# Recommendation tower: gram products in two bursts a tile, a GpSimd wait three chunks ahead, eleven look-ups in every unit, last unit tile by tile

## The reference, cut to what matters

```python
# ids [2048, 27]; 27 tables of 128 columns (1000 to 125000 rows)
e = stack([tbl_f[ids[:, f]] for f in range(27)], axis=1)      # [2048, 27, 128]
z = einsum('bnd,bmd->bnm', e, e)[:, c, r]                     # 351 pairs below the diagonal
h = concatenate([z, dense_ctx], axis=1)                       # [2048, 367]
h = maximum(h @ W_top1 + b_top1, 0)                           # 512 columns
h = maximum(h @ W_top2 + b_top2, 0)                           # 256 columns
y = h @ W_top3                                                # [2048, 1]
```

## Time and profile before

| | |
|---|---|
| time, median of 3 runs | 360.29 us (360.21 to 361.26) |
| profiled execution, first to last instruction | 358.7 us |
| TensorE matmuls busy | 333.7 us, 93% |
| VectorE busy | 246.3 us, 69% |
| GpSimd busy | 250.4 us, 70% |
| ScalarE busy | 144.4 us, 40% |
| mean granted TensorE clock | 0.986 of full speed |

### The profile page before, as it was taken

How to read it: one execution, slowest core, us unless ns; L and a number is a source line. 1 busy time by engine, 2 the same in 40 slices (tenths; PEclk the granted TensorE clock), 3 DMA queues, 4 the chain that set the end, 5 groups by cost and what they waited for, 6 DMA issues and landing times.

```text
span 358.7 us, 13616 instructions
## 1 busy us (share of the span) xinstructions
PE 333.7 (93%) x6094; PEld 303.4 (85%) x6094; DVE 246.3 (69%) x329; ACT 144.4 (40%) x265; POOL 250.4 (70%) x271
## 2 busy tenths in 40 slices
PE   1879699989999989999999999999999999999896
PEld 0779499978999979898889989999899989997775
DVE  3959979975488935878197965968387955961142
ACT  2536524444433433335343453435343353435320
POOL 5777777777777777777777777777777777777200
PEclk9969989999999999999999999999999999999999
DMA  6997744534333353443333452434533443322100
GB/s 184 306 318 196 205 136 107 102 93 91 83 93 82 90 99 75 96 96 80 93 88 82 115 85 77 105 84 81 102 89 83 99 98 74 84 55 55 27 3 1
DMA packets 26155, 36.86 MB, mean 103 GB/s; under 512 B 8451, under 2 KB 20099, under 8 KB 26098
## 3 DMA queue, kind: packets, MB, share of 16 engines
q0 software_dynamic: 8448, 17.32, 20.5%
q1 hardware_dynamic: 17506, 18.16, 20.1%
q10 hardware_dynamic: 144, 0.52, 0.4%
HBM read 35.97 MB, written 0.01 MB: 100 GB/s over the span
## 4 chain that ended last, share of the span: by engine, by line
PE 57%; POOL 26%; issue 10%; DVE 3%; DMA 3%; ACT 1%; DVEq 0%; ACTq 0%
POOL rows L450 26%; PE e_banks L482 25%; PE w_banks L543 9%; PE g_banks L513 8%; PE w_banks L554 7%; PE e_banks L494 6%; DMA rows<-in_tbl,idx 2%; DVE one_hot L672 2%; PE w_banks L532 1%; DVE zt L686 1%; DMA idx<-in_idx 1%; ACT et L340 0%; ACT h L333 0%; ACT et L350 0%; DVE a L720 0%
## 5 line engine op out<-in xcount | busy, mean ns | idle before, releaser
L450 POOL DMA_INDIRECT rows<-in_tbl,idx x264 | 249.6, 945 | 82.9 <-issue 78.0
L672 DVE TENSOR_TENSOR one_hot<-ids_wide,row_no 128x1024 fp32r<-128x1024 int32 x160 | 186.3, 1215 | 76.5 <-PE e_banks L482 72.5
L482 PE MATMUL e_banks<-one_hot,table_hi 128*128 128x256 f32 x672 | 172.2, 294 | 3.4 <-issue 3.4
L482 PE MATMUL e_banks<-one_hot,table_lo 128*128 128x256 f32 x672 | 167.0, 287 | 0.0
L482 PEld LDWEIGHTS e_banks<-one_hot,table_hi 128*128 128x128 f32 x672 | 131.4, 196 | 4.4 <-issue 4.2
L482 PEld LDWEIGHTS e_banks<-one_hot,table_lo 128*128 128x128 f32 x672 | 131.6, 196 | 0.2
L350 ACT ACTIVATE et<-e_banks 128x256 f32<-128x256 f32 x84 | 57.9, 689 | 89.3 <-PE e_banks L482 89.3
L340 ACT ACTIVATE et<-e_banks 128x512 f32<-128x512 f32 (+1 forms) x68 | 45.0, 664 | 52.3 <-PE e_banks L494 51.5
L513 PEld LDWEIGHTS g_banks<-et 128*26 128x26 f32 x4096 | 41.7, 103 | 17.7 <-issue 13.3
L513 PE MATMUL g_banks<-et 128*26 128x26 f32 x4096 | 50.0, 191 | 1.8 <-DVE zt L686 1.3
L494 PE MATMUL e_banks<-ident,rows 128*128 128x128 f32 x264 | 43.0, 285 | 5.5 <-DMA rows<-in_tbl,idx 5.5
(11 more groups left out here) (25 smaller groups left out, 67.7 us busy)
## 6 DMA issues: line engine op xcount, KB each, us to landing
ids_wide<-in_ids SPq DMA_DIRECT2D x80, 128.0 KB
et<-in_kept_tables SPq DMA_DIRECT2D x10, 512.0 KB, 10.1
rows<-in_tbl,idx POOLq DMA_INDIRECT x264
et<-in_kept_tables ACTq DMA_DIRECT2D x1, 512.0 KB, 3.9
a1T<-in_ids SPq DMA_DIRECT2D x4, 128.0 KB, 10.8
w<-in_w SPq DMA_DIRECT2D x2, 256.0 KB
w<-in_W_top SPq DMA_DIRECT2D x1, 512.0 KB
w<-in_w SPq DMA_DIRECT2D x1, 222.0 KB
```

The costliest lines, as they stand in the source:

```text
L450: pool.indirect_dma_start(rows[:, k % RING, a, :], None, tables[f], bass.IndirectOffsetOnAxis(ap=idx[:, t, f:f + 1], axis=0)).then_inc(row ...
L482: last = nc.tensor.matmul(e_bank[n % E_BANKS][:, 0:UNIT], part[:, q, c, :], one_hot[:, hot_slot(o, piece), c % PIECE, :], start=(c == 0 an ...
L672: nc.vector.tensor_tensor(one_hot[:, hot_slot(o, piece), :, :], ids_place(o).unsqueeze(1).broadcast_to([P, PIECE, UNIT]), row_no[:, piece ...
```

## The change

Tile t's eight gram pieces are issued as two bursts of four, at the end of the first and the third tick of tile t+1 (for tile 14 the first and the second), instead of a pair in every tick. Each burst raises `g_filled` once, and the turn waits for both. `H` steps are interleaved with look-ups and layer steps now.

GpSimd, before it gathers chunk k, waits until the transposes of chunk k-4 and all bursts that lie in ticks up to k-4 are done. The ring keeps its seven places.

`GATHERED_IN` is empty: 256 gathers, 64 chunks of four, 88 look-ups. The costs and the first tick of each unit's look-ups change, so look-ups move between ticks.

The last unit's layers are done tile by tile. Layer 1 of unit 6 is one tick, its layer 2 the next; tile 14's turning and layer 1 (`H1`, `M1`, 128 columns each) lie in the last tick. `END` holds tile 15's grams with tile 14's layer 2 between the bursts, and then tile 15's own turning, layer 1 and layer 2. For tile 15, ScalarE and VectorE take the drains in turn.

```diff
-GATHERED_IN = {0: 3, 4: 1}
+GATHERED_IN = {}
+AHEAD_BY = 3
@@ the order
-        at = 1 + (n - AHEAD) * 7 // 10
-        step = [("OH", 0, q)] + [("HI", n + AHEAD)]
+        at = 1 + (n - AHEAD) * 6 // 10
+        step = [("OH", 0, q)] + [("HI", m) for m in range(n + AHEAD, min(n + AHEAD + 1, NOH))]
...
+    HALF = G_PIECES // 2
+    BURST_AT = []
     for t in range(LAST_TILE):
         at = TILE_AT[t + 1] + (t == 0)
-        for p in range(G_PIECES):
-            step = [("G", t, p)] + ([("turn", t), ("pack", t)] if p == G_PIECES - 1 else [])
-            grams[at + p * 4 // G_PIECES].append(step)
-    for u in range(LAST):
-        at, then = TILE_AT[PAIR * (u + 1) + 1], TILE_AT[min(PAIR * (u + 2), LAST_TILE)]
+        for half, tick in enumerate((at, at + (1 if t == LAST_TILE - 1 else 2))):
+            grams[tick] += [("G", t, p) for p in range(half * HALF, (half + 1) * HALF)]
+            BURST_AT.append(tick)
+        grams[tick] += [("turn", t), ("pack", t)]
+    for u in range(LAST - 1):
+        at, then = TILE_AT[PAIR * (u + 1) + 1], TILE_AT[PAIR * (u + 2)]
         turns[at] += [[("H", u, c)] for c in range(KC)]
         layers[at + 1] += [[("L1", u, 0)], [("L1", u, 1)]]
         layers[at + 2] += [[("L1", u, 2)], [("L1", u, 3)]]
-        if u < LAST - 1:
-            layers[then].append([("L2", u, 0)])
-            layers[then + 1].append([("L2", u, 1)])
-
-    COLUMNS = {"T": 1024, "OH": 4096, "G": 1024, "H": 1024, "L1": 3072, "L2": 4096}
-    LOOK_UPS_FROM = [0, TILE_AT[1] + 1] + [TILE_AT[PAIR * (u - 1)] + 4 for u in range(2, UNITS + 1)]
+        layers[then + 1].append([("L2", u, 0)])
+        layers[then + 2].append([("L2", u, 1)])
+
+    at, tile = TILE_AT[LAST_TILE], LAST_TILE - 1
+    turns[at] += [[("H", LAST - 1, c)] for c in range(KC)]
+    layers[at + 1] += [[("L1", LAST - 1, m)] for m in range(M1)]
+    layers[at + 2] += [[("L2", LAST - 1, j)] for j in range(PAIR)]
+    layers[at + 3] += [[("H1", tile, c)] for c in range(KC)] + [[("M1", tile, m)] for m in range(M1)]
+
+    COLUMNS = {"T": 1024, "OH": 4608, "G": 768, "H": 768, "L1": 3072, "L2": 4096, "H1": 320, "M1": 1536}
+    LOOK_UPS_FROM = [0, TILE_AT[1] + 2] + [TILE_AT[PAIR * (u - 1)] + 3 for u in range(2, UNITS)] + [TILE_AT[LAST_TILE]]
...
-    END = pieces[:G_PIECES // 2] + [("L2", LAST - 1, 0)] + pieces[G_PIECES // 2:] \
-        + [("turn", LAST_TILE), ("pack", LAST_TILE), ("L2", LAST - 1, 1)] \
-        + [("H", LAST, c) for c in range(KC)] + [("L1", LAST, m) for m in range(M1)] \
-        + [("L2", LAST, j) for j in range(PAIR)]
+    END = pieces[:HALF] + [("L2", LAST, 0)] + pieces[HALF:] + [("turn", LAST_TILE), ("pack", LAST_TILE)] \
+        + [("H1", LAST_TILE, c) for c in range(KC)] + [("M1", LAST_TILE, m) for m in range(M1)] \
+        + [("L2", LAST, PAIR - 1)]
...
-        for step in look_ups[k] + layers[k]:
-            STEPS += step
-        for turn, piece in itertools.zip_longest(turns[k], grams[k], fillvalue=[]):
-            STEPS += turn + piece
+        for turn, step in itertools.zip_longest(turns[k], look_ups[k] + layers[k], fillvalue=[]):
+            STEPS += turn + step
+        STEPS += grams[k]
@@ GpSimd
-                if k >= RING:
-                    pool.wait_ge(t_filled, k - RING + 1)
+                if k > AHEAD_BY:
+                    pool.wait_ge(t_filled, k - AHEAD_BY)
+                bursts = sum(tick <= k - AHEAD_BY - 1 for tick in BURST_AT)
+                if bursts:
+                    pool.wait_ge(g_filled, bursts)
@@ TensorE
-                if p == G_PIECES - 1:
+                if p % HALF == HALF - 1:
                     last.then_inc(g_filled, 1)
...
+            def turn_tile_pairs(s):
+                _, t, c = s
+                n = W_AT[s]
+                free_w_bank(n)
+                wait_packed(t, c)
+                nc.tensor.transpose(w_bank[n % WB][0:KROWS[c], 0:P], h[:, t % PAIR, c * P:c * P + KROWS[c]], ident[:]
+                                    ).then_inc(w_filled, 1)
+
+            def layer1_tile(s):
+                _, t, m = s
+                n = W_AT[s]
+                free_w_bank(n)
+                for c in range(KC):
+                    if m == 0:
+                        w_emptied(W_AT["H1", t, c])
+                    last = nc.tensor.matmul(w_bank[n % WB][:, 0:P], w1[0:KROWS[c], c, m * P:(m + 1) * P],
+                                            hT[0:KROWS[c], c, t % PAIR, :],
+                                            start=(c == 0), stop=(c == KC - 1))
+                last.then_inc(w_filled, 1)
@@ VectorE
-                dve.wait_ge(g_filled, t + 1)
+                dve.wait_ge(g_filled, 2 * (t + 1))
```

More of the change, by code:

```diff
@@ L150, in dlrm_tower @@
         layers[at + 2] += [[("L1", u, 2)], [("L1", u, 3)]]
-        if u < LAST - 1:
-            layers[then].append([("L2", u, 0)])
-            layers[then + 1].append([("L2", u, 1)])
-    COLUMNS = {"T": 1024, "OH": 4096, "G": 1024, "H": 1024, "L1": 3072, "L2": 4096}
-    LOOK_UPS_FROM = [0, TILE_AT[1] + 1] + [TILE_AT[PAIR * (u - 1)] + 4 for u in range(2, UNITS + 1)]
-    load = [sum(COLUMNS[step[0][0]] for step in turns[k] + layers[k] + grams[k]) for k in range(TICKS)]
+        layers[then + 1].append([("L2", u, 0)])
[7 more added lines that the diff above has]
+    LOOK_UPS_FROM = [0, TILE_AT[1] + 2] + [TILE_AT[PAIR * (u - 1)] + 3 for u in range(2, UNITS)] + [TILE_AT[LAST_TILE]]
+    load = [COLUMNS["T"] + sum(COLUMNS[step[0]] for part in turns[k] + layers[k] + [grams[k][:HALF]] for step in part)
+            for k in range(TICKS)]
     for u in range(1, UNITS):
@@ L328, in w_engine, with turned_cols, layer1_cols @@
                 return "dve"
-            return "dve" if s[1] == LAST and s[2] % 2 == 1 else "act"
+            return "dve" if s[1] == LAST_TILE and s[0] in ("H1", "M1") and s[2] % 2 == 1 else "act"
+        def turned_cols(s):
+            if s[0] == "H":
+                return w_bank[W_AT[s] % WB][:, 0:UNIT].rearrange("p (j b) -> p j b", b=P), slice(0, PAIR)
+            j = s[1] % PAIR
+            return w_bank[W_AT[s] % WB][:, 0:P].unsqueeze(1), slice(j, j + 1)
+        def layer1_cols(s):
+            if s[0] == "L1":
+                return w_bank[W_AT[s] % WB][:, 0:UNIT].rearrange("p (j b) -> p j b", b=P), slice(0, PAIR)
+            j = s[1] % PAIR
+            return w_bank[W_AT[s] % WB][:, 0:P].unsqueeze(1), slice(j, j + 1)
         def copy(eng, out, src):
@@ L612, in drain_turned @@
                 act.wait_ge(w_filled, n + 1)
-                cols = w_bank[n % WB][:, 0:UNIT].rearrange("p (j b) -> p j b", b=P)
-                copy("act", hT[0:KROWS[c], c, :, :], cols[0:KROWS[c]]).then_inc(w_drained[n % WB], 1)
+                cols, tiles = turned_cols(s)
+                copy("act", hT[0:KROWS[c], c, tiles, :], cols[0:KROWS[c]]).then_inc(w_drained[n % WB], 1)
             def drain_layer1(s):
@@ L645, in _ @@
                     pack_first(s[1])
-                elif s[0] == "H" and w_engine(s) == "act":
+                elif s[0] in ("H", "H1") and w_engine(s) == "act":
                     drain_turned(s)
-                elif s[0] == "L1" and w_engine(s) == "act":
+                elif s[0] in ("L1", "M1") and w_engine(s) == "act":
                     drain_layer1(s)
@@ L749, in _ @@
                     pack_rest(s[1])
-                elif s[0] == "H" and w_engine(s) == "dve":
+                elif s[0] in ("H", "H1") and w_engine(s) == "dve":
                     drain_turned(s)
-                elif s[0] == "L1" and w_engine(s) == "dve":
+                elif s[0] in ("L1", "M1") and w_engine(s) == "dve":
                     drain_layer1(s)
```

22 lines of the change are left out of this document (14 added, 8 removed).

## The result

The changed kernel takes 368.13 us (median of 5 runs, 364.90 to 369.96) against 360.29 (5 runs, 360.20 to 361.26): ratio 1.0207, 95% interval 1.0176 to 1.0237. It is slower, as the whole interval lies above 1; whether by more than 2% stays open. The forecast was 357 us and faster, and the time lies outside the range of 352.5 to 363.

What follows compares the result with a forecast made beforehand. TensorE, busy 93%, and GpSimd, gathering without a stop, were taken as all but balanced, TensorE a little behind. 358.7 + 0.3 + 0.7 - 4.1 = 355.6 us span; median 1.6 above, 357.2; range 352.5 to 363.

Steps and rivals of the forecast that it cites:

- gaps: I take the middle, 5.0: Tile 2 to last chunk: gaps inside 28 bursts total 5.0 us against 3 before, +2.0; bounds 0 and 14.3.
- Rival 1: Bursts run dry: each long burst has 0.51 us of gaps, 14.3 instead of 5.0; time 366.5 us, slower; chance 0.14.
- Joining saves 0.23 a burst: Gram pieces: one burst of four costs 1.29 us where two pairs cost 1.52.
- To tile 2, 65.2: Start to tile 2's transposes: 64.9 us before, changes sum to +0.3, so tile 2 at 65.2.
- Waits for rows and around `H`, -3.9: Tile 2 to last chunk: row waits of 2.6 us and about 1.3 around H steps end, -3.9.
- The new wait, hidden: GpSimd loses about 5.9 us at chunks 9, 11 and 12, hidden by TensorE being later; then gathers without a stop.
- The end, 18.5: Last chunk's transposes to kernel end: 18.5 us against 22.6 before, -4.1, with last-unit records at 0.113 us.
- The end's sign: Last unit by tile: end gains 4.1 us, while unit 6's layer 2 moved into the middle costs 3.5.
- Look-ups, +5.8 here and one more ahead: Tile 2 to last chunk: 72 look-ups instead of 69, 1.92 us each, +5.8; before tile 2, one fewer, -1.92.
- Rival 3: A burst saves nothing, since each matmul has a fixed price; time 361.6 us; chance 0.08.
- Rival 4: Last unit by tile gives nothing, M1 being as dear as L1; time 361.5 us, no difference; chance 0.08.
- Rival 2: Gathers bound the kernel: gaps are small and the rows' landing sets the end; time 353 to 356 us; chance 0.20.

Runs made afterwards that it cites:

- e6: Not the kernel's computation: TensorE alternates 24 matmuls with bursts of 256 gram records on constant data, GpSimd idle, gathering or doing something else; span 167.0 us.
- e7: Gram records alone on constant data: bursts of 64, 96 and 128 with GpSimd idle, then 128 beside gathers, plain DMAs or memsets; span 236.6 us.
- e3: Changed kernel without gathers: each chunk's rows come by one plain SyncE DMA of fixed table 0 rows; 355.38 us, 0.9878 of the kernel before.
- e9: Kernel before with only the last unit done tile by tile, tile 14's grams put in three ticks; 363.72 us, 1.0119.
- e10: e9 with tile 14's layer 2 behind the last turn, unit 6's second layer 2 between the last bursts, ScalarE draining all H1; 363.75 us, 1.0100.
- e12: Kernel before with only GpSimd's new wait (transposes and gram bursts of earlier ticks) added; 360.66 us, 1.0004.
- e13: Changed kernel run again unaltered for a second profile; this execution took 363.36 us.
- e11: Kernel before with only eleven look-ups in every unit (four more look-ups, eight gathers fewer); 365.74 us, 1.0139.
- e4: Changed kernel without GpSimd's new wait, ring only as before; 366.39 us median, 1.0142 from the three quickest executions; the profiled one took 372.86 us.
- e15: Changed kernel run again unaltered for another profile; this execution took 370.52 us.
- e16: Changed kernel run again unaltered for another profile; this execution took 370.10 us.
- e2: Kernel before with only the grams in bursts of four pieces in two ticks and its three H steps in a row; 375.12 us, 1.0432.

## Why the prediction was wrong

**The term that failed is "gaps: I take the middle, 5.0".** It came out at 11.9 us in the 28 bursts of the middle, or 0.43 each; the bounds were 0 and 0.51. By the prediction's own sum, 271.9 + 6.9 gives 278.8 for the middle; measured were 279.3. From the forecast of 357.2 us to the 364.9 of the profiled execution the parts are -2.3 to tile 2, +7.4 in the middle and +2.5 at the end; the other 3.2 us, to the median of 368.1, are the spread (below). The 3 us taken for gaps in the kernel before were near: its profile has 2.6. The choice of 5.0 rested on two bursts, at 338.76 without a gap and at 341.88 with one. Both lie behind the last gather at 333.08, so neither shows what happens beside a gather. The gap of the second lies at instruction 12225, which is 193 of a block, and TensorE went on 2.5 us after a packet of instructions began (e6 shows what that means): it is of the other kind, and that the small ones, 0.43 a burst, come near the 0.51 taken from it is chance. What brings the gap is shown three ways: the four bursts without gathers in the changed kernel (1.08 us), e7's stage (1.33 to 1.74 beside gathers, 1.08 without), and e3, where the gathers are gone and the time is 12.75 us less. Rival 1 had nearly the size (0.51 a burst, 366.5 us), from a sample of the other kind; its chance of 0.14 was too small for a case that one of two samples spoke for.

Step by step, the rest:

- *Joining saves 0.23 a burst*: right, 0.22. From the look-up matmul ahead of it to the transpose behind it a pair takes 0.87 us before the change and a burst without a gap 1.41 in e3; less the 0.12 that one matmul takes anyway, two pairs are 1.51 and a burst 1.29.
- *To tile 2, 65.2*: came out at 62.9, by 2.3 earlier. At least part of it is a thing that was not in the sum. The kernel before has the clock granted at half there, and the changed kernel, in three profiles of five, has not. e9 and e10 have the order of before up to there: e9, with the full clock in this stretch, reached tile 2 at 63.8, e10, with half, at 66.9. The kernel before, by stretch:

```profile
47.00:51.00 4.00, 4.00 (x23) 3.87 (x21) 3.31 (x3) 0.70 (x1) 3.09 (x4) 0.58 0.35 99
```

- *Waits for rows and around `H`, -3.9*: right. Nothing above 0.7 us is left in the middle.
- *The new wait, hidden*: right. GpSimd lost time at chunks 9, 11 and 12 as forecast (its gathers stand at 51.90, 63.71 and 69.81), leads were 8.6 to 12 us in the middle and 6.0 at tick 61; e12 has 1.0004. That GpSimd would then gather without a stop was wrong: it also stood still for 1.0 to 1.5 us in each of the chunks 22, 28, 38, 46 and 54, at no cost.
- *The end, 18.5*: 21.0. Layer 1 by tile has records of 0.125 to 0.128 us where I took 0.113, and it starts once all blocks are there and not a third ahead: e13, at full clock, has 19.7, so these make 1.2. The half clock of the second layer 1 makes the rest, 1.3.
- *The end's sign*: the sum had it at -4.1 and layer 2 of unit 6 at +3.5 in the middle, -0.6 in all. e9 shows +4.3. Moving a layer 2 step into the middle is paid in full there, and the gain of the end is 2.4. Of the 5.5 that the middle of e9 lost, 3.5 are layer 2 and 0.8 a pair of grams moved ahead of the last chunk; e9 waits 3.2 us for rows, against 2.6. The rest of some 0.6 I can't place. The ratio is 2.3 above what the two profiles show (360.7 and 358.7); most of that is that e9's profile is of its shortest span, where the others have 361.4 to 363.3.
- *Look-ups, +5.8 here and one more ahead*: right in the sum. They were to be paid by what bursts and waits give back; e11 has them alone at +5.0, 2.0 of which is a wait of its own.

**The parts, measured alone**: new end +1.19%, look-ups +1.39% (0.8% without e11's own wait), wait +0.04%. Together 2.6%, or 2.1% less that wait, against 2.07% of the whole. If the parts add up, that leaves -0.5% to 0 for the bursts and the moved `H` steps; the intervals added as squares are ±0.7%. So the two parts that cost are the ones that the bursts were to pay for, and the bursts pay nearly nothing that can be told from zero.

**The spread.** Of nine executions of the changed kernel three lie at 363.4 to 364.9 us and six at 367.7 to 370.5, where no execution of before is above 362. Two of the six were seen in a trace, and both have the stop at record 111 with half clock behind it, which none of the three below 365 has. That the other four have it too is likely and not shown. The forecast had no such thing in it. By rival 1 the time was 366.5, and at the quick end of the spread the kernel is still 0.9% slower than before.

On instruction supply the Trainium skill (Runtime: NRT & Kernel Launch, "Instruction fetch mechanics") says that blocks of 256 instructions are fetched ahead, and that the fetch is hidden since the sequencer issues more slowly than the blocks arrive. The trace agrees with the blocks: one packet comes for each 256 instructions. That the fetch is hidden does not hold here: 128 gram records are 256 instructions with their weight loads, used up in 1.08 us, and one packet took 0.88 to 1.67 us in the profiles of the changed kernel (median 1.0), and where TensorE stopped it went on 2.2 us or more after the packet began.

**Rival 3**, a burst saves nothing, is out: joining saves the 0.22 above, and 128 records in 1.08 us are 8.5 ns each. **Rival 4**, a tile's layer 1 as dear as a unit's, is out too: 0.125 to 0.128 us a record against 0.217. **Rival 2** was the bound that I took for near. e3 lies at 355.4, within its 353 to 356, but by another road, without gathers.

## What to carry to other kernels

The price of a stretch of very short matmuls can depend on what other engines do beside it and on where it lies in the instruction stream; take a sample from a place with the same neighbours, and treat samples from the tail, where GpSimd has gone quiet, as another population. When a few parts of a change are to pay for others, time each alone: here the saving was the doubtful part and the costs were sure. And take more than one profile when the executions of a kernel spread by 2%: the first profile was of the quickest one and did not hold the largest single loss of the others.

## What the runs showed of the hardware

- GpSimd's gathers (indirect DMAs) stop TensorE's stream of short matmuls twice in each 1.25 us, mostly for 0.2 to 0.29 us; its plain DMAs and memsets do not. The one-hot look-ups show nothing of it. By what path it happens is open: no run separates the making of descriptors from the rest of a gather.
- A run of gram records can stop for 0.2 to 2.9 us at one place in every 256 of TensorE's instructions, and goes on 2.2 to 3.0 us after a 16 KB packet began on the instruction queue (45 stops above 0.3 us). Of bursts with 128 records three of 24 did in e7, not counting those beside gathers; of those with 256 all 18 in e6. In the changed kernel such stops come at the same four places, two of them in all five profiles; how long each lasts differs between executions.
- In four of five stops above 2 us in the kernels (two in e4, one each in e15 and e16), the clock was granted at half for 3.4 us, from 0.2 to 1.4 us after TensorE had gone on; in e15 that cost 1.5 us more. After the fifth, of 2.24 us in e2, it stayed full.
